# Expert rows of a mixture-of-experts layer: VectorE moves the gathered rows, and the weighted rows get a second buffer

## The chip, the cores and the metric

The kernel runs on one core of a Trainium2 chip. The metric is the device time of one execution in microseconds; the median of three runs is quoted, and beside it one execution that the hardware profiler recorded.

## What is computed

One layer on x, 64 x 64 tokens of 256 numbers (4096 tokens, 32 tiles of 128): cross attention, causal self attention, and a mixture of 8 experts of which each token uses 2, each with its residual. The part that matters here is the last:

```python
logits_BSE = jnp.einsum('BSD,DE->BSE', x, router_kernel_DE)
probs_BSE = jax.nn.softmax(logits_BSE.astype(jnp.float32), axis=-1)
weights_BSK, indices_BSK = jax.lax.top_k(probs_BSE, TOP_K)           # TOP_K = 2 of 8
norm_weights_BSK = jax.nn.softmax(weights_BSK, axis=-1)
...
act_BSEF = jax.nn.silu(jnp.einsum('BSD,EDF->BSEF', x, kernel_gating_EDF))   # D = 256, F = 512
fuse_BSEF = act_BSEF * jnp.einsum('BSD,EDF->BSEF', x, kernel_up_EDF)
down_BSED = jnp.einsum('BSEF,EFD->BSED', fuse_BSEF, kernel_down_EFD)
out_BSD = jnp.einsum('BSED,BSE->BSD', down_BSED, full_weights_BSE)
```

## The kernel before

Both attentions and the router come first and are not touched. After them the tokens are sorted by expert: `token_of` holds, column by column, the token numbers of each tile of 128 rows that one expert handles. There are 67 such tiles, at least 5 for each expert. The expert part then runs over these tiles.

What one tile i needs, in the order of its data:

- a **gather** on GpSimd's queue (`gather(i)`, L1375): an indirect DMA that brings 128 rows of `xn` (256 normalised numbers and the token's 8 expert weights, ROW = 264) from DRAM into one of two buffers `xs_in`. Two small GpSimd instructions stand ahead of it: `token_now` (L1372) copies the tile's token numbers, `dummy` (L1374) waits for that copy.
- a **move** on GpSimd (`move(i)`, L1383 and L1386): the 8 weights go to `slot_weights`, the 256 numbers to the single buffer `e_xs`. The move waits until TensorE has transposed the tile before (`xt_mm`).
- TensorE transposes `e_xs` into `e_xt_ps` (`turn_x(i)`, L1429); ScalarE and VectorE split it into a rounded part and a remainder (`e_xt_hi`, `e_xt_lo`).
- TensorE makes gate and up (`gate_up(i)`, `e_g_ps`, `e_u_ps`, 12 matmuls of 512 columns), ScalarE the silu, VectorE the product `e_h`.
- TensorE transposes `e_h` (`turn_h(i)`, `e_ht_ps`), which is split again (`e_ht_hi`, `e_ht_lo`), and makes the down product `e_y_ps` (`down(i)`, 12 matmuls of 256 columns).
- ScalarE's `y_copy(i)` (L1500) multiplies it by the weights into the single buffer `e_ys`. It waits until the scatter of the tile before has landed (`s_added`), since that scatter reads the buffer.
- a **scatter** on GpSimd's queue (`add_rows(i)`, L1396): an indirect DMA that adds the 128 rows to `acc` in DRAM. `token_out` (L1391) and `out_gate` (L1395) stand ahead of it. Scatters must not overlap, as two experts can add to one row: `token_out` waits for the landing of the scatter before, `out_gate` for `y_copy(i)`.

Each engine works through its own instructions in the order written; semaphores tie them together. TensorE's unit is a step: `step(i)` is turn_x(i+1), turn_h(i-1), gate_up(i), down(i-1). ScalarE's and VectorE's unit is `tile(i)`, with the work that belongs to that step. In the first three steps of each expert but the last, `tile` also splits a third of the next expert's weights (`e_w_hi` on ScalarE, `e_w_lo` on VectorE); when the third is done, the SyncE queue loads the raw weights of the expert after next (three DMAs of 512 KB). GpSimd's loop takes two tiles a turn; for each tile n it does move(n), gather(n+2), add_rows(n-3).

Of the kernel before, what the change touches and what calls it, by code (L numbers as in the profile page):

```python
# [16 lines left out]
ALU = mybir.AluOpType  # L17
# [5 lines left out]
P = 128  # L23
HEAD = 64
MIN_TILES = 5
# [958 lines left out]
def moe(nc, sem, sbuf, psum, xn_sb, xn_dram, s_xn_stored, ident, r_hi, r_lo, w_gate, w_up, w_down, acc,  # L984
# [23 lines left out]
    with ExitStack() as ph:  # L1008
# [288 lines left out]
        with ExitStack() as ex:  # L1297
# [6 lines left out]
            xs_in = [sbuf(ex, f"e_xs_in{i}", [P, ROW]) for i in range(2)]  # L1304
            xs_sb = sbuf(ex, "e_xs", [P, D])
# [6 lines left out]
            ys_sb = sbuf(ex, "e_ys", [P, D])  # L1312
# [54 lines left out]
            def _(pool):  # L1367
                def gather(i, half):


                    wait(pool, s_moved, i - 1 if isinstance(i, int) else i + -1)
                    nc.gpsimd.tensor_tensor(token_now[half][:], token_of[:, bass.ds(i, 1)], none[:], ALU.add).then_inc(s_now, 1)  # L1372
                    pool.wait_ge(s_now, i + 1)
                    nc.gpsimd.tensor_tensor(dummy[half][:], zero[:], zero[:], ALU.add).then_inc(s_dummy, 1)  # L1374
                    pool.indirect_dma_start(  # L1375
                        out=xs_in[half][:], out_offset=None, in_=xn_dram,
                        in_offset=bass.IndirectOffsetOnAxis(ap=token_now[half][:], axis=0)).then_inc(s_xs[half], DMA)

                def move(i, pair, half):

                    pool.wait_ge(s_xs[half], DMA * pair + DMA)
                    wait(pool, s_dummy, i)
                    nc.gpsimd.tensor_tensor(weight[:, bass.ds(i * EXPERTS, EXPERTS)], xs_in[half][:, D:ROW],  # L1383
                                            zero[:].to_broadcast([P, EXPERTS]), ALU.add).then_inc(s_weight, 1)
                    wait(pool, xt_mm, i)
                    nc.gpsimd.tensor_tensor(xs_sb[:], xs_in[half][:, 0:D], zero[:].to_broadcast([P, D]), ALU.add).then_inc(s_moved, 1)  # L1386

                def add_rows(i):
# [8 lines left out]
                        out=acc, out_offset=bass.IndirectOffsetOnAxis(ap=token_out[:], axis=0), in_=ys_sb[:],  # L1397
# [5 lines left out]
                for half in range(2):  # L1403
                    gather(half, half)
                for half in range(2):
                    move(half, 0, half)
                    gather(2 + half, half)
                for half in range(2):
                    move(2 + half, 1, half)
                    gather(4 + half, half)  # L1410
                add_rows(0)
                with pool.Fori(2, more_pairs) as j:
                    for half in range(2):
                        move(2 * j + half, j, half)
                        gather(2 * j + (2 + half), half)
                        add_rows(2 * j + (half - 3))
# [170 lines left out]
```

## Time and profile before

| | us |
|---|---|
| median of 3 runs (lowest, highest) | 2474.48 (2471.78, 2474.54) |
| the profiled execution | 2472.68 |
| its span, first to last instruction | 2470.9 |
| first GpSimd gather, from the span's start | 2060.36 |
| last scatter, from the span's start | 2451.66 |
| last instruction of all, the copy of `acc` to the output | from 2455.55 |

Times in the views below count from the span's start. The expert part, to which the change is confined, is the stretch from 2060 on, some 400 us of the span; all ahead of it is the same in both kernels. "Busy" is the time an engine executed; a duration on GpSimd (POOL) can begin while the instruction before it is still at work, so that its length holds a wait. For a DMA that GpSimd issues, the duration of the instruction is the making of its descriptors, and the rows land later.

### The profile page before, as it was taken

To read this page: it belongs to the slowest core of one execution; us is meant where nothing else is said; L and a number is where in the kernel's file an instruction comes from. 1 tells how busy PE (TensorE), PEld (TensorE's weight loads), DVE (VectorE), ACT (ScalarE), POOL (GpSimd) and SP (SyncE) were. 2 spreads that over 40 slices of the span, in tenths; PEclk is the share of its full clock that TensorE was granted. 3 is DMA by queue.
4 is the path that set the end of the run, shared out by engine and by line. 5 is a ranking of instruction groups with operands and counts; after the bars stand their busy time and mean duration, and the time that the engine had idled before them with its cause. 6 is when DMAs were issued, how large, how long until landed. Compare 5 with 4: busy or idle time off the path is not lost. (4 is left out here: it accounts for less than half of the span.)

```text
span 2470.9 us, 53415 instructions
## 1 busy us (share of the span) xinstructions
PE 2315.3 (94%) x18144; PEld 1993.0 (81%) x18144; DVE 1533.7 (62%) x3324; ACT 1266.8 (51%) x3832; POOL 900.9 (36%) x1141
## 2 busy tenths in 40 slices
PE   6999999999999999999997999999999956998895
PEld 5888888888888888888886889999999844777775
DVE  5656665656565655665555888888888765433332
ACT  4555454545554554555554666666666522433332
POOL 3333333333233323333332222222222224877784
PEclk9999999999999999999998999999999977999998
DMA  5000000000000000000001000000000012334334
GB/s 169 18 10 17 15 10 10 15 17 8 17 8 17 8 17 8 17 8 17 8 1 69 1 18 9 17 17 8 17 8 18 18 37 78 72 74 97 73 48 98
DMA packets 52934, 73.94 MB, mean 30 GB/s; under 512 B 9408, under 2 KB 36800, under 8 KB 52800
## 3 DMA queue, kind: packets, MB, share of 16 engines
q1 hardware_dynamic: 39952, 55.07, 7.0%
q0 software_dynamic: 12912, 17.98, 4.4%
q8 instruction: 38, 0.62, 0.1%
q14 instruction: 32, 0.26, 0.0%
HBM read 55.47 MB, written 21.76 MB: 31 GB/s over the span
## 5 line engine op out<-in xcount | busy, mean ns | idle before, releaser
L356 POOL TENSOR_TENSOR p_sb<-p_sb,rinv 128x512 f32<-128x512 f32 x256 | 283.7, 1108 | 874.0 <-DVE rinv L601 874.0
L523 ACT ACTIVATE p_sb<-s_ps,nmax 128x256 f32<-128x256 f32 x512 | 237.9, 469 | 411.1 <-DVE nmax L582 411.1
L744 POOL TENSOR_TENSOR sp_sb<-sp_sb,srinv 128x512 f32<-128x512 f32 x128 | 133.2, 1041 | 441.7 <-DVE srinv L930 441.7
L57 DVE TENSOR_TENSOR kt_lo<-k_ps,kt_hi 128x512 fp32r<-128x512 f32 x256 | 176.0, 687 | 140.3 <-ACT kt_hi L45 137.6
L58 DVE SCALAR_TENSOR_TENSOR qbd_lo<-m_ps,qbd_hi 64x256 fp32r<-64x256 f32 x256 | 108.0, 422 | 226.9 <-ACT qbd_hi L46 225.2
L45 ACT CAST kt_hi<-k_ps 128x512 fp32r<-128x512 f32 x256 | 150.9, 590 | 169.5 <-PE k_ps L65 169.5
L598 DVE COPY pt_sb<-t_ps 128x512 f32<-128x512 f32 x256 | 176.7, 690 | 43.1 <-PE t_ps L449 39.2
L878 ACT ACTIVATE sp_sb<-sm_sb,snmax 128x128 f32<-128x128 f32 x512 | 199.4, 390 | 6.4 <-DVE snmax L941 3.3
L463 PE MATMUL o_ps<-pt_sb,v_sb 128*64 128x64 f32 x4096 | 175.5, 228 | 0.2 <-DVE pt_sb L598 0.2
L463 PEld LDWEIGHTS o_ps<-pt_sb,v_sb 128*64 128x64 f32 x4096 | 140.1, 137 | 43.5 <-issue 43.2
L582 DVE TENSOR_REDUCE nmax<-s_ps 128x2 f32<-128x512 f32 x256 | 173.9, 679 | 0.0
L57 DVE TENSOR_TENSOR e_ht_lo<-e_ht_ps,e_ht_hi 128x512 fp32r<-128x512 f32 x67 | 46.3, 691 | 187.4 <-ACT e_ht_hi L45 183.3
L449 PEld LDWEIGHTS t_ps<-ident,p_sb 128*128 128x128 f32 x1024 | 127.7, 141 | 34.6 <-issue 0.8
L449 PE MATMUL t_ps<-ident,p_sb 128*128 128x128 f32 x1024 | 153.8, 273 | 0.9 <-DVE pt_sb L598 0.5
L543 ACT COPY v_sb<-v_ps 128x512 f32<-128x512 f32 x256 | 149.7, 585 | 4.8 <-PE v_ps L65 1.7
L65 PE MATMUL s_ps<-kt_hi,qbd_hi 128*128 128x256 f32 x512 | 144.0, 281 | 3.1 <-issue 2.1
L65 PE MATMUL s_ps<-kt_hi,qbd_lo 128*128 128x256 f32 x512 | 144.7, 283 | 0.0
L65 PE MATMUL s_ps<-kt_lo,qbd_hi 128*128 128x256 f32 x512 | 144.6, 282 | 0.0
L65 PE MATMUL k_ps<-cx_hi,wk_hi 128*128 128x512 f32 x256 | 125.9, 492 | 13.1 <-DVE wk_lo L57 8.1
L46 ACT ACTIVATE sqt_hi<-sqk_ps 128x256 fp32r<-128x256 f32 x128 | 49.1, 384 | 155.0 <-PE sqk_ps L65 155.0
L1500 ACT ACTIVATE e_ys<-e_y_ps,slot_weights 128x256 f32<-128x256 f32 x67 | 31.8, 474 | 176.0 <-DMA acc<-e_ys,e_token_out 176.0
L1396 POOL DMA_INDIRECT acc<-e_ys,e_token_out x67 | 107.4, 1603 | 24.2 <-issue 21.4
(278 smaller groups left out, 7607.9 us busy)
## 6 DMA issues: line engine op xcount, KB each, us to landing
ctx_raw<-in_ctx_t SPq DMA_DIRECT2D x32, 256.0 KB, 2.7
ctx_raw<-in_ctx_t SPq DMA_DIRECT2D x64, 128.0 KB, 2.8
xn<-f_xn SPq DMA_DIRECT2D x16, 256.0 KB, 2.2
acc<-x_sb SPq DMA_DIRECT2D x16, 256.0 KB, 2.3
e_raw<-in_gate SPq DMA_DIRECT2D x8, 512.0 KB
e_raw<-in_up SPq DMA_DIRECT2D x8, 512.0 KB
e_raw<-in_down SPq DMA_DIRECT2D x8, 512.0 KB
x_sb<-in_x SPq DMA_DIRECT2D x1, 3584.0 KB, 13.6
```

Source lines behind the costliest of these rows:

```text
L45: return nc.scalar.copy(hi, src)
L57: return nc.vector.tensor_tensor(lo, src, f32(hi), ALU.subtract)
L65: mm = pe.matmul(out, lhs, rhs, start=(i == 0), stop=(i == len(pairs) - 1))
L356: nc.gpsimd.tensor_tensor(prob, prob, inv, ALU.mult).then_inc(norm_done, 1)
L449: mm = pe.transpose(t_ps[:, k * P:(k + 1) * P], p_sb[:, (p - 3) % 4, k * P:(k + 1) * P], ident[:])
L463: mm = pe.matmul(o_ps[h * HEAD:(h + 1) * HEAD, (2 * w + b) * HEAD:(2 * w + b + 1) * HEAD], v_sb[:, k, q * P + h * HEAD:q * P + (h + 1) * H ...
L523: ex = nc.scalar.activation(p_sb[:, k, b * J:(b + 1) * J], s_ps[1 - w][:, b * J:(b + 1) * J], ACT.Exp, bias=nmax[:, k, b:b + 1], scale=1.0 ...
L543: nc.scalar.copy(v_sb[:, p % 4, p // 4 * HALF:(p // 4 + 1) * HALF], v_ps[:]).then_inc(v_done, 1)
L582: nc.vector.tensor_reduce(nmax[:, (p - 1) % 4, :], s_ps[1 - w][:].rearrange("p (b j) -> p b j", b=2), AX_X, ALU.max, negate=True).then_inc ...
L598: nc.vector.tensor_copy(pt_sb[:, 1 - w, :], t_ps[:]).then_inc(t_done, 1)
L744: nc.gpsimd.tensor_tensor(prob, prob, inv, ALU.mult).then_inc(norm_done, 1)
L878: ex = nc.scalar.activation(p_sb[:, s, k * P:(k + 1) * P], sm_sb[:, w, k * P:(k + 1) * P], ACT.Exp, bias=nmax[:, s, k:k + 1], scale=1.0, a ...
```

## The change

- GpSimd's move is gone. VectorE does it (`move(i)`, L1513 to L1521 after): one copy of all 264 columns from `xs_in` to `e_xs`, which now has room for the weights. It waits for the gather's landing, for TensorE's transposes of the tile before, and for ScalarE to have taken the weights of the tile before. It is the last thing VectorE does for a step ahead of any weight split: `tile(i)` ends with move(i+2).
- ScalarE copies the 8 weights from `e_xs` to `slot_weights` behind `e_xt_hi` (L1473).
- `e_ys` is two buffers in turn. `y_copy(i)` no longer waits for the landing of scatter i-1, but for `token_out` of tile i-1, which is behind the landing of scatter i-2.
- GpSimd's loop does, for each tile n, gather(n), add_rows(n-3), where before it was move(n), gather(n+2), add_rows(n-3). Four gathers stand ahead of the loop's first add_rows, where before there were six.

```diff
--- before.py
+++ after.py
@@ -1301,15 +1301,15 @@
             none = sbuf(ex, "e_none", [P, 1], mybir.dt.uint32)
             dummy = [sbuf(ex, f"e_dummy{i}", [P, 1]) for i in range(2)]
             token_out = sbuf(ex, "e_token_out", [P, 1], mybir.dt.uint32)
-            xs_in = [sbuf(ex, f"e_xs_in{i}", [P, ROW]) for i in range(2)]
-            xs_sb = sbuf(ex, "e_xs", [P, D])
+            xs_in = sbuf(ex, "e_xs_in", [P, 2 * ROW])
+            xs_sb = sbuf(ex, "e_xs", [P, ROW])
             xt_hi = sbuf(ex, "e_xt_hi", [P, D], F32R)
             xt_lo = sbuf(ex, "e_xt_lo", [P, D], F32R)
             silu_sb = sbuf(ex, "e_silu", [P, F])
             h_sb = sbuf(ex, "e_h", [P, F])
             ht_hi = sbuf(ex, "e_ht_hi", [P, F], F32R)
             ht_lo = sbuf(ex, "e_ht_lo", [P, F], F32R)
-            ys_sb = sbuf(ex, "e_ys", [P, D])
+            ys = sbuf(ex, "e_ys", [P, 2 * D])
             xt_ps = psum(ex, "e_xt_ps")
             g_ps = psum(ex, "e_g_ps")
             u_ps = psum(ex, "e_u_ps")
@@ -1365,27 +1365,19 @@
             @block.gpsimd
             def _(pool):
-                def gather(i, half):
-
-
-                    wait(pool, s_moved, i - 1 if isinstance(i, int) else i + -1)
+                def gather(i, half, freed):
+
+
+                    wait(pool, s_moved, freed)
                     nc.gpsimd.tensor_tensor(token_now[half][:], token_of[:, bass.ds(i, 1)], none[:], ALU.add).then_inc(s_now, 1)
                     pool.wait_ge(s_now, i + 1)
+                    wait(pool, s_dummy, i)
                     nc.gpsimd.tensor_tensor(dummy[half][:], zero[:], zero[:], ALU.add).then_inc(s_dummy, 1)
                     pool.indirect_dma_start(
-                        out=xs_in[half][:], out_offset=None, in_=xn_dram,
+                        out=xs_in[:, half * ROW:(half + 1) * ROW], out_offset=None, in_=xn_dram,
                         in_offset=bass.IndirectOffsetOnAxis(ap=token_now[half][:], axis=0)).then_inc(s_xs[half], DMA)
-                def move(i, pair, half):
-
-                    pool.wait_ge(s_xs[half], DMA * pair + DMA)
-                    wait(pool, s_dummy, i)
-                    nc.gpsimd.tensor_tensor(weight[:, bass.ds(i * EXPERTS, EXPERTS)], xs_in[half][:, D:ROW],
-                                            zero[:].to_broadcast([P, EXPERTS]), ALU.add).then_inc(s_weight, 1)
-                    wait(pool, xt_mm, i)
-                    nc.gpsimd.tensor_tensor(xs_sb[:], xs_in[half][:, 0:D], zero[:].to_broadcast([P, D]), ALU.add).then_inc(s_moved, 1)
-
-                def add_rows(i):
+                def add_rows(i, half):
                     wait(pool, s_added, DMA * i)
                     nc.gpsimd.tensor_tensor(token_out[:], token_of[:, bass.ds(i, 1)], none[:], ALU.add).then_inc(s_out_now, 1)
@@ -1394,31 +1386,28 @@
                     wait(pool, s_out_gate, i)
                     nc.gpsimd.tensor_tensor(out_gate[:], zero[:], zero[:], ALU.add).then_inc(s_out_gate, 1)
                     pool.indirect_dma_start(
-                        out=acc, out_offset=bass.IndirectOffsetOnAxis(ap=token_out[:], axis=0), in_=ys_sb[:],
+                        out=acc, out_offset=bass.IndirectOffsetOnAxis(ap=token_out[:], axis=0), in_=ys[:, half * D:(half + 1) * D],
                         in_offset=None, compute_op=ALU.add).then_inc(s_added, DMA)
                 more_pairs = pool.value_load(pairs[0:1, 0:1], min_val=MIN_TILES * EXPERTS // 2, max_val=MAX_TILES // 2)
                 nc.gpsimd.memset(none[:], 0).then_inc(s_zero, 1)
                 pool.wait_ge(s_zero, 2)
-                for half in range(2):
-                    gather(half, half)
-                for half in range(2):
-                    move(half, 0, half)
-                    gather(2 + half, half)
-                for half in range(2):
-                    move(2 + half, 1, half)
-                    gather(4 + half, half)
-                add_rows(0)
+                for i in range(4):
+                    gather(i, i % 2, i - 1)
+                add_rows(0, 0)
                 with pool.Fori(2, more_pairs) as j:
                     for half in range(2):
-                        move(2 * j + half, j, half)
-                        gather(2 * j + (2 + half), half)
-                        add_rows(2 * j + (half - 3))
+                        gather(2 * j + half, half, 2 * j + (half - 1))
+                        add_rows(2 * j + (half - 3), 1 - half)
+                left = pool.value_load(first_left[0:1, 0:1], min_val=MIN_TILES * EXPERTS - 4, max_val=MAX_TILES - 4)
                 for half in range(2):
-                    move(2 * more_pairs + half, more_pairs, half)
-                not_added = pool.value_load(first_left[0:1, 0:1], min_val=MIN_TILES * EXPERTS - 4, max_val=MAX_TILES)
-                with pool.Fori(not_added, tile_count(pool)) as i:
-                    add_rows(i)
+                    gather(left + (3 + half), half, left + (2 + half))
+                with pool.Fori(left + 5, tile_count(pool) + 2) as i:
+                    gather(i, 0, left + 4)
+                for k in range(3):
+                    add_rows(left + k, 1 - k % 2)
+                with pool.Fori(left + 3, tile_count(pool)) as i:
+                    add_rows(i, 0)
             @block.tensor
             def _(pe):
@@ -1481,6 +1470,7 @@
                     act.wait_ge(xt_mm, i + 1)
                     wait(act, u_mm, i)
                     split_hi_act(nc, xt_hi[:], xt_ps[:, 0:D]).then_inc(xt_h, 1)
+                    nc.scalar.copy(weight[:, bass.ds(i * EXPERTS, EXPERTS)], xs_sb[:, D:ROW]).then_inc(s_weight, 1)
                 def rest(i):
@@ -1495,9 +1485,8 @@
                 def y_copy(i, e):
                     act.wait_ge(y_mm, i + 1)
-                    act.wait_ge(s_weight, i + 1)
-                    wait(act, s_added, DMA * i)
-                    nc.scalar.activation(ys_sb[:], y_ps[:, 0:D], ACT.Copy,
+                    wait(act, s_out_now, i)
+                    nc.scalar.activation(ys[:, bass.ds((i % 2) * D, D)], y_ps[:, 0:D], ACT.Copy,
                                          scale=weight[:, bass.ds(i * EXPERTS + e, 1)]).then_inc(y_copied, 1)
                 def tile(i, before, e, e_before, piece):
@@ -1522,6 +1511,15 @@
             @block.vector
             def _(dve):
+                def move(i):
+
+                    half = i % 2
+                    dve.wait_ge(s_xs[0], DMA * (i // 2) + DMA)
+                    wait(dve, s_xs[1], DMA * ((i + 1) // 2))
+                    wait(dve, s_weight, i)
+                    wait(dve, xt_mm, i)
+                    nc.vector.tensor_copy(xs_sb[:], xs_in[:, bass.ds(half * ROW, ROW)]).then_inc(s_moved, 1)
+
                 def xt_lo_copy(i):
                     dve.wait_ge(xt_h, i + 1)
                     split_lo_dve(nc, xt_lo[:], xt_ps[:, 0:D], xt_hi[:]).then_inc(xt_l, 1)
@@ -1540,14 +1538,18 @@
                     ht_lo_copy(before)
                     product(i)
                     xt_lo_copy(i + 1)
+                    move(i + 2)
                     if piece is not None:
                         dve.wait_ge(s_whi, PIECES * (e + 1) + piece + 1)
                         cut = slice(piece * CUT, (piece + 1) * CUT)
                         split_lo_dve(nc, w_lo[:, (e + 1) % 2, cut], raw[:, cut], w_hi[:, (e + 1) % 2, cut]).then_inc(s_wlo, 1)
+                move(0)
                 xt_lo_copy(0)
+                move(1)
                 product(0)
                 xt_lo_copy(1)
+                move(2)
                 last = run_tiles(dve, tile)
                 ht_lo_copy(last)
```

The order of GpSimd's instructions in the loop, for the first of a turn's two tiles (n = 2j), before. `e_xs_in` is the landing buffer, `e_xs` the moved rows; a row that only waits or computes an address reads ISA or REGISTER_ALU:

```order
L1383 ISA [waits e_dummy_done]
L1383 TENSOR_TENSOR slot_weights<-e_xs_in,e_zero 128x8
L1386 TENSOR_TENSOR e_xs<-e_xs_in,e_zero 128x256 [waits e_xt_mm]
L35 REGISTER_ALU
L1372 ISA [waits e_xs_moved]
L1372 TENSOR_TENSOR e_token_now<-token_of,e_none 128x1
L1373 REGISTER_ALU
L1374 TENSOR_TENSOR e_dummy<-e_zero 128x1 [waits e_token_now_set]
L1375 DMA e_xs_in<-xn,e_token_now 128x264
L35 ISA
L1391 ISA [waits e_ys_added]
```

And after, from the first row of the loop's body to the wait for the y of tile n-3 and its scatter:

```order
L1372 ISA [waits e_xs_moved]
L1372 TENSOR_TENSOR e_token_now<-token_of,e_none 128x1
L1373 REGISTER_ALU
L1375 TENSOR_TENSOR e_dummy<-e_zero 128x1 [waits e_dummy_done,e_token_now_set]
L1376 DMA e_xs_in<-xn,e_token_now 128x264
L35 ISA
L1383 ISA [waits e_ys_added]
L1383 TENSOR_TENSOR e_token_out<-token_of,e_none 128x1
L1384 REGISTER_ALU
L1387 TENSOR_TENSOR e_out_gate<-e_zero 128x1 [waits e_out_gate_done,e_y_weighted,e_token_out_set]
L1388 DMA acc<-e_ys,e_token_out 4224x256
```

The gather in the loop was that of tile n+2 and stood behind the move of tile n; it is now that of tile n, and stands directly behind the scatter of tile n-4, which is the last row of the turn before.

VectorE's instructions of a step without weight pieces, before:

```order
L57 TENSOR_TENSOR e_ht_lo<-e_ht_ps,e_ht_hi 128x512 [waits e_ht_hi_done]
L1530 REGISTER_ALU
L1533 TENSOR_TENSOR e_h<-e_u_ps,e_silu 128x512 [waits e_ht_mm,e_silu_done,e_u_mm]
L1526 REGISTER_ALU
L57 TENSOR_TENSOR e_xt_lo<-e_xt_ps,e_xt_hi 128x256 [waits e_xt_hi_done]
```

And after:

```order
L1531 TENSOR_TENSOR e_h<-e_u_ps,e_silu 128x512 [waits e_ht_mm,e_silu_done,e_u_mm]
L1524 REGISTER_ALU
L57 TENSOR_TENSOR e_xt_lo<-e_xt_ps,e_xt_hi 128x256 [waits e_xt_hi_done]
L1517 ISA
L35 ISA [waits e_xs_loaded0]
L1521 ISA [waits e_xt_mm,e_weight_kept,e_xs_loaded1]
L1521 COPY e_xs<-e_xs_in 128x264
```

The copy, with two waiting rows of its own, now stands between `e_xt_lo` and the next step's `e_ht_lo`.

## Rows read from the trace of the kernel before

**Rows 1.** GpSimd's timeline (start us, us, what, idle before): scatters of tiles 2, 64.
```profile
2092.38 1.59 POOL L1396 DMA_INDIRECT acc<-e_ys,e_token_out  x1 [0.15 <-issue]
...
2441.22 1.55 POOL L1396 DMA_INDIRECT acc<-e_ys,e_token_out  x1 [0.48 <-issue]
```

**Rows 2.** Windows: us; PE, PEld, DVE, ACT, POOL busy; PEclk, DMA share, GB/s.
```profile
2300.00:2400.00 100.00, 90.72 (x536) 76.13 (x534) 38.24 (x60) 38.92 (x77) 79.76 (x145) 1.00 0.35 64
2430.00:2456.00 26.00, 16.30 (x95) 13.84 (x93) 5.83 (x10) 6.37 (x14) 11.04 (x18) 0.90 0.26 31
```

**Rows 3.** TensorE's timeline, one early step, and the next one's start.
```profile
2079.76 0.38 PE L1429 MATMUL e_xt_ps<-ident,e_xs 128*128 128x128 f32 x2
...
2084.48 0.28 PE L65 MATMUL e_y_ps<-e_w_lo,e_ht_hi 128*128 128x256 f32 x1
2084.59 0.38 PE L1429 MATMUL e_xt_ps<-ident,e_xs 128*128 128x128 f32 x2
```

**Rows 4.** GpSimd's timeline, one tile.
```profile
2206.15 1.61 POOL L1396 DMA_INDIRECT acc<-e_ys,e_token_out  x1 [0.48 <-issue]
2207.22 0.78 POOL L1383 TENSOR_TENSOR slot_weights<-e_xs_in,e_zero 128x8 f32 x1
2207.38 1.19 POOL L1386 TENSOR_TENSOR e_xs<-e_xs_in,e_zero 128x256 f32<-128x256 f32 x1
2208.75 0.19 POOL L1372 TENSOR_TENSOR e_token_now<-token_of,e_none 128x1 uint32<-128x1 uint32 x1 [0.19 <-POOL e_xs L1386]
...
2209.55 1.00 POOL L1375 DMA_INDIRECT e_xs_in<-xn,e_token_now  x1 [0.33 <-issue]
2210.57 0.20 POOL L1391 TENSOR_TENSOR e_token_out<-token_of,e_none 128x1 uint32<-128x1 uint32 x1
2210.84 0.20 POOL L1395 TENSOR_TENSOR e_out_gate<-e_zero 128x1 f32<-128x1 f32 x1
2211.51 1.60 POOL L1396 DMA_INDIRECT acc<-e_ys,e_token_out  x1 [0.48 <-issue]
```

**Rows 5.** The chain that ended last, in order of time: start, us, what.
```profile
2425.26 1.60 POOL acc L1396
2426.86 0.24 POOL slot_weights L1383
...
2428.62 2.76 DMA e_xs_in<-xn,e_token_now
...
2435.99 3.81 DMA acc<-e_ys,e_token_out
```

**Rows 6.** ScalarE's timeline within the stretch of rows 4.
```profile
2210.20 0.47 ACT L1500 ACTIVATE e_ys<-e_y_ps,slot_weights 128x256 f32<-128x256 f32 x1 [2.66 <-DMA acc<-e_ys,e_token_out]
```

**Rows 7.** Waits from 2100 to 2400: us in total, times, longest.
```profile
ACT e_ys L1500 <- DMA acc<-e_ys,e_token_out: 142.5, 53, 5.4
```

**Rows 8.** VectorE's groups by form: busy, mean ns of one.
```profile
L185 DVE TENSOR_SCALAR ln_xn_x<-x_sb,ln_mv_x,ln_rstd_x 128x256 f32 x28 | 20.4, 772 | 0.0
...
L185 DVE TENSOR_SCALAR ln_xn_s<-x_sb,ln_mv_s,ln_rstd_s 128x256 f32 x24 | 8.7, 406 | 0.0
```

**Rows 9.** VectorE's timeline at the step of rows 3.
```profile
2084.02 0.41 DVE L57 TENSOR_TENSOR e_xt_lo<-e_xt_ps,e_xt_hi 128x256 fp32r<-128x256 f32 x1
```

**Rows 10.** GpSimd's timeline: a gather with nothing late ahead of it.
```profile
2076.08 0.19 POOL L1372 TENSOR_TENSOR e_token_now<-token_of,e_none 128x1 uint32<-128x1 uint32 x1
...
2076.68 0.97 POOL L1375 DMA_INDIRECT e_xs_in<-xn,e_token_now  x1
```

**Rows 11.** The chain that ended last, at two of the expert weight loads.
```profile
2060.36 5.55 DMA e_xs_in<-xn,e_token_now
...
2228.40 6.38 DMA acc<-e_ys,e_token_out
```

**Rows 12.** VectorE's and GpSimd's timelines at a weight piece.
```profile
2224.87 1.45 DVE L57 TENSOR_TENSOR e_w_lo<-e_raw,e_w_hi 128x1024 fp32r<-128x1024 f32 x1 [0.38 <-ACT e_w_hi L45]
...
2225.39 0.97 POOL L1372 TENSOR_TENSOR e_token_now<-token_of,e_none 128x1 uint32<-128x1 uint32 x1 [0.17 <-POOL e_xs L1386]
```

## The prediction

> **What bounds the kernel now.** The times by step come first. The expert part is one pipeline over 67 tiles, so I read it at its pace. Between the starts of the scatters of tiles 2 and 64 lie 2441.22 - 2092.38 = 348.84 us for 62 tiles, 5.63 us each [rows 1]. The windows say how hard each engine works in there: in 100 us TensorE is busy 90.7 and GpSimd 79.8, VectorE 38 and ScalarE 39, at a granted clock of 1.00, which is TensorE's upper level, 2.4 GHz [rows 2]. TensorE looks like the bound, but its own work is shorter than the pace: in an early step, when the first gathers had run ahead, it goes from one `turn_x` to the next in 2084.59 - 2079.76 = 4.83 us [rows 3]. So some 0.8 us a tile is waiting, about 50 us over the part, and that is the most that any relief could give.
>
> GpSimd's timeline says what sets the pace. From one scatter to the next, 2206.15 to 2211.51, it runs one instruction behind the other: scatter, the two moves, `token_now`, `dummy`, gather, `token_out`, `out_gate`, scatter, in 5.36 us [rows 4]. The "busy" 80% is an undercount, since the rest is hand-over between its own instructions, 0.2 to 0.5 us at a time. Beside it stands a ring through the single `e_ys`: the scatter lands 3.81 us after its start [rows 5], and only then may ScalarE write the next `e_ys`, from which the next scatter starts 2211.51 - 2210.20 = 1.31 us later [rows 4, 6]. That makes 5.1 to 5.3 us, nearly the same pace; it is what the 142.5 us of waiting ahead of `e_ys` are [rows 7]. Both must be relieved for a gain, and the change relieves both.
>
> **What is removed.** The moves leave GpSimd. Their real end is 2208.57 (2207.38 + 1.19), and the scatter ahead of them is done at 2207.76 [rows 4], so they occupy about 0.8 us, and with the wait on them ahead of `token_now` about 1 us. GpSimd's round would be 5.36 - 1.0 = 4.4 us. The ring no longer holds `e_ys`: landing, `token_out`, `out_gate`, scatter, which is 3.81 + about 0.1 + (2211.51 - 2210.57 = 0.94) = 4.85 us at most. Both lie at TensorE's 4.83.
>
> **What is added on VectorE and ScalarE.** VectorE gets one copy of 128x264 a tile, from SBUF to SBUF. The trace has no such copy. The nearest row is a VectorE operation of 128x256 f32 with an SBUF source and no second tensor, 406 ns; the same operation takes 772 ns in the stage where something holds it up [rows 8]. Below, a copy at twice the element rate would be some 0.2 us. I take 0.35 and keep 0.2 and 0.77 for the range. The Trainium skill ("VectorE: DVE Perf Modes", section "Mode 2×_2P") says that an fp32 copy between SBUF tensors handles two elements per cycle; by its clock and its overheads that is an estimate of 0.2 to 0.3 us, and the sum would be some 3 us lower by it. No row here shows such a copy.
>
> The copy stands behind `e_xt_lo`, which ends at 2084.02 + 0.41 = 2084.43, 0.16 before TensorE starts the next `turn_x` at 2084.59 [rows 3, 9]. With the copy and a hand-over of 0.15 TensorE could start at 2084.93: 0.33 us late. So even with every gather early the pace would be 4.83 + 0.33 = 5.16, not 4.83. ScalarE's copy of 8 weights (about 0.2 us) lies between `e_xt_hi` and `y_copy` while TensorE is still at the down product, 1.4 us; I cost it at nothing. With the weight pieces, 21 of 67 steps, that cover is used up and it would cost its 0.2 us each, 4 us at most.
>
> **What is moved: the gather.** This decides, in my reading. Before, GpSimd did gather(n+2) in the round of tile n, so a gather stood behind the scatter of a tile six before its own, and its landing was never late. After, gather(n) is in the round of tile n, directly behind scatter n-4. That scatter waits in `out_gate` for y_copy(n-4), and y_copy(n-4) for the down product of tile n-4, which is the last work of TensorE's step n-3. The gathered rows are wanted by turn_x(n) at the start of step n-1. So only step n-2 lies between the event that frees the gather and the moment its rows are needed, and the way from one to the other is long. Link by link, from the end of the down product:
>
> - hand-over to ScalarE 0.15 (as from ScalarE to GpSimd: 2210.84 less 2210.67 = 0.17 [rows 4, 6]);
> - start of y_copy to start of the scatter 1.31 [rows 4, 6];
> - the scatter's descriptors 1.60, and the first small instruction behind it 0.24 [rows 5]; here that is `token_now`;
> - end of `token_now` to the start of the gather, 2076.68 - 2076.27 = 0.41, as nothing late stands ahead [rows 10];
> - start of the gather to its landing 2.76 [rows 5];
> - hand-over to VectorE 0.15, the copy 0.35, hand-over to TensorE 0.15.
>
> The sum is L = 7.12 us. TensorE then needs, from the start of that step to the end of its down product, 2084.48 + 0.28 - 2079.76 = 5.00 us [rows 3]. The loop closes over two steps: end of step n-3, L, start of step n-1, 5.00, end of step n-1. So two steps take 7.12 + 5.00 = 12.12 us, and the pace is 6.06, if nothing else is slower. TensorE will wait for the moved rows 1.2 us a step on the mean, likely short and long by turns, since a step that follows a long wait finds its own gather nearly there.
>
> Against 5.63 now that is 0.43 us a tile more, over 62 tiles 27 us. Three smaller terms. The loads of expert weights, one for each of 7 experts, stretch what is under way beside them: a gather from 2.76 to 5.55 us and a scatter from 3.81 to 6.38 [rows 5, 11]. The pace of before holds such delays already; the 6.06 does not. As the two interleaved chains can absorb part of a delay, I add 1 us for each, under half of the 2.6 to 2.8: 6 us. The weight pieces: while VectorE makes `e_w_lo`, a GpSimd instruction of 0.19 us takes 0.97 [rows 10, 12]. Before, that was in the 5.63 as well; afterwards it falls on the chain above in part of the 21 cases, 0.8 us at every fourth or fifth: 3 us. At the ends something is saved: the first move is 0.35 instead of about 0.8, and for the last tiles no gather is left, so the ring of 4.85 instead of 5.2 holds for three scatters, and the start is a little quicker: -5 us. The sum is 27 + 6 + 3 - 5 = 31 us. The profiled execution took 2472.68 us, 1.8 below the median of the runs; 2472.7 + 31 = 2503.7, and I say 2503.
>
> **The rivals.** A measurement of this kernel can tell about 0.2%, 5 us, from no change.
>
> *The gather is in time* (faster; 0.10). What speaks for it is what the diff removes, since both limits of before go. Then VectorE's late copy sets 5.16: 62 x 0.47 = 29 us less, 2444. It needs a way from down product to rows of at most 5.3 us, where I count 7.12; the descriptors of scatter and gather and the landing alone are 1.60 + 2.76 = 4.36. The point from which it turns: at L = 6.26 the pace equals today's, at about 5.8 the other terms are paid too and the kernel is faster by more than 5 us.
>
> *Late, but for no more than was lost before* (no change; 0.07). L near 6.1 to 6.2 gives a pace of 5.55 to 5.6, and 2470 to 2479 with the smaller terms. It would take hand-overs of 0.05 us, a copy of 0.2 and a gather that lands 2.3 us after its start.
>
> *VectorE's copy holds GpSimd off* (slower still; 0.15). When TensorE has waited, the copy falls 1.4 to 1.8 us after the end of the down product, which is when GpSimd starts the scatter's descriptors. VectorE and GpSimd do get in each other's way at `e_w_lo`, 0.19 against 0.97 us [rows 10, 12]. If each copy adds its 0.35 to L, the pace rises by 0.17, 11 us in all: 2514. The Trainium skill speaks against this change here: "SBUF — State Buffer", section "SBUF: two separate sides", has it that an fp32 copy from SBUF to SBUF on VectorE keeps GpSimd from writing descriptors while it runs. The row agrees for an operation with two SBUF inputs, and shows nothing for a copy.
>
> *TensorE's clock* (0.08). With a wait of 1.2 us a step TensorE is busy 4.83 of 6.06, 80%. At 63% busy (16.3 of 26 us, in the last tiles) the clock granted was 0.90; at 91% it was 1.00 [rows 2]. If it were 0.95 throughout, the 5.00 in the loop would be 5.26: 62 x 0.13 = 8 us more, 2511.
>
> **The numbers.** The late gather as summed has 0.60; with the two rivals that lie above it, 0.83 are slower. Its ends: a gather landing after 2.4, a copy of 0.2 and hand-overs of 0.1 make L = 6.46, a pace of 5.73, +6 us, and with half of the small terms 2480. A copy of 0.77, a landing of 3.1 and 0.35 for the hold-off make L = 8.23, 6.6 and +61, which all at once is unlikely; two of the three give about 2528. The forecast's own range is 2486 to 2522. For 8 in 10 I give 2476 to 2530, which leaves out the faster rival and the far upper end.
>
> **What would show it.** In the changed profile: the pace of scatters about 6.06 us; TensorE's largest wait in the part that for `e_xs` by VectorE (1 to 1.3 us a step), and behind it VectorE's copy waiting for the gather's DMA, about as long; GpSimd waiting in `out_gate` for ScalarE's `e_ys`; hardly any wait of `e_ys` for a landing. If instead VectorE's copy waits for `e_xt_lo` alone and the pace is 5.2, the gather was in time and I am wrong. Wrong too would be a pace of 6 with the chain leading through landings of scatters.

## The result, and the profile after

The changed kernel takes 2564.96 us (2561.35 to 2570.36) against 2474.16 (2471.78 to 2474.54) for the kernel before on the same chip. The ratio is 1.0371, with an interval of 1.0349 to 1.0393: slower by about 91 us. The forecast was 2503 us, so the direction was right and the size a third of what came.

GpSimd's timeline after (columns as in [rows 1]), the scatters of tiles 2 and 64:

```profile
2091.87 1.59 POOL L1388 DMA_INDIRECT acc<-e_ys,e_token_out  x1 [0.15 <-issue]
...
2539.54 1.59 POOL L1388 DMA_INDIRECT acc<-e_ys,e_token_out  x1 [0.50 <-issue]
```

447.67 us for 62 tiles is 7.22 us a tile, where [rows 1] gave 5.63. That is 98.8 us more, so the whole loss lies in the pace of the expert part: the two profiled executions, 2472.68 and 2570.36, are 97.7 apart.

The two rows of the waits from 2100 to 2500 that matter (engine, what it waited for: us in total, times, longest):

```profile
PE e_xt_ps L1418 <- DVE e_xs L1521: 78.2, 29, 5.0
DVE e_xs L1521 <- DMA e_xs_in<-xn,e_token_now: 70.3, 28, 5.0
```

TensorE waits for VectorE's copy of the gathered rows, and VectorE for the gather to land. The number of times is what to read: 29 and 28 in some 56 steps. Every second step waits, for 78.2 / 29 = 2.7 us, and the others hardly at all. The 142.5 us of `e_ys` for a landing [rows 7] have no row any more.

The same on TensorE's timeline, where each row is a `turn_x`, the start of a step:

```profile
2306.14 0.68 PE L1418 MATMUL e_xt_ps<-ident,e_xs 128*128 128x128 f32 x2 [2.29 <-DVE e_xs L1521]
...
2312.73 0.43 PE L1418 MATMUL e_xt_ps<-ident,e_xs 128*128 128x128 f32 x2
...
2320.18 0.43 PE L1418 MATMUL e_xt_ps<-ident,e_xs 128*128 128x128 f32 x2 [2.35 <-DVE e_xs L1521]
...
2325.40 0.43 PE L1418 MATMUL e_xt_ps<-ident,e_xs 128*128 128x128 f32 x2
```

Two steps do the same work, and both follow a wait of 2.3 us. The one from 2320.18 takes 5.22, the one from 2306.14 takes 6.59. The windows say why (us; PE, PEld, DVE, ACT, POOL busy; granted clock, DMA share, GB/s): first four of 100 us each, then the stretch of those steps, with what lies between left out:

```profile
2100.00:2200.00 100.00, 80.74 (x399) 68.60 (x400) 33.44 (x58) 33.62 (x72) 46.96 (x80) 0.84 0.30 66
2200.00:2300.00 100.00, 83.54 (x422) 70.20 (x421) 31.80 (x59) 32.29 (x73) 46.31 (x83) 0.86 0.28 53
2300.00:2400.00 100.00, 80.59 (x425) 68.56 (x424) 35.94 (x63) 36.10 (x77) 49.43 (x85) 0.90 0.27 53
2400.00:2500.00 100.00, 79.54 (x425) 67.79 (x424) 32.08 (x60) 33.20 (x74) 48.71 (x86) 0.90 0.28 53
...
2306.00:2309.00 3.00, 2.86 (x10) 2.57 (x11) 0.68 (x2) 0.59 (x1) 2.46 (x4) 0.50 0.41 49
2310.00:2313.00 3.00, 2.96 (x20) 2.53 (x19) 1.45 (x4) 1.98 (x5) 0.00 (x0) 1.00 0.00 0
...
2320.00:2324.00 4.00, 3.83 (x21) 3.29 (x22) 1.97 (x4) 1.24 (x3) 2.92 (x5) 1.00 0.39 51
```

TensorE has stood still for 2.3 us; then the granted clock is 0.50, which is its lower level of 1.2 GHz, for the next 3 us. It is back at 1.00 by 2310. Behind the wait that ends at 2320 it does not fall. The kernel before had 1.00 throughout this part and 0.90 only at its end [rows 2]. Of the 400 us here, (0.16 + 0.14 + 0.10 + 0.10) / 0.5 x 100 = 100 us were at the lower level. In windows of 2 us over 2090 to 2550 it is 109 us, with TensorE busy for 97 of them. Half of that work time, 48 us, is a first estimate of what the clock cost. Counted on TensorE's timeline it is a little less: from the step at 2099.99 on, 32 steps follow a wait of 1.9 us or more, and 27 of them take 6.4 to 7.8 us from their start to the end of their down product, where all other steps take 5.1. The excess of the 27 adds up to 45 us.

The chain of waits over one long wait of TensorE (start, us, what). It follows the end of the down product, 2312.69, and ScalarE's `e_ys`, which starts at 2312.96:

```profile
2313.57 0.52 POOL e_out_gate L1387
...
2314.28 0.06 POOL acc L1388
...
2315.36 0.74 POOL e_token_now L1372
...
2316.51 2.74 DMA e_xs_in<-xn,e_token_now
...
2319.28 0.11 DVEq L35
...
2319.44 0.05 DVEq L35
...
2319.54 0.11 DVEq L1521
...
2319.70 0.35 DVE e_xs L1521
...
2320.18 0.43 PE e_xt_ps L1418 x2
```

This is the way that the prediction counted out, link for link: gate, scatter, `token_now`, gather, landing, copy, `turn_x`.

### The profile page after: what moved, and what is told of

Its sections match the earlier page's. It is cut to its first block and busy times, and to the rows that moved or that the text cites. A ratio compares the mean times of both kernels' runs of the same rounds, so it can differ in the third digit from the quotient of the medians.

```text
span 2568.6 us, 53602 instructions
## 1 busy us (share of the span) xinstructions
PE 2359.1 (92%) x18144; PEld 2031.0 (79%) x18144; DVE 1551.7 (60%) x3393; ACT 1285.3 (50%) x3900; POOL 838.6 (33%) x1008
## 5 line engine op out<-in xcount | busy, mean ns | idle before, releaser
L1418 PE MATMUL e_xt_ps<-ident,e_xs 128*128 128x128 f32 x136 | 33.9, 336 | 101.4 <-DVE e_xs L1521 99.2
L1531 DVE TENSOR_TENSOR e_h<-e_u_ps,e_silu 128x512 f32<-128x512 f32 x67 | 46.3, 691 | 130.9 <-PE e_u_ps L65 130.9
L1388 POOL DMA_INDIRECT acc<-e_ys,e_token_out x67 | 106.7, 1593 | 30.0 <-issue 29.4
```

## The experiments

All times are medians, each with the kernel before timed beside it; "ratio" is the time over that of the kernel before, with its 95% interval. The diffs are cut to the lines that matter, and "..." marks where lines were left out.

### The gather one tile earlier

Everything of the change is kept; only the gather is brought forward in GpSimd's order.

```
-                for i in range(4):
+                for i in range(5):
                     gather(i, i % 2, i - 1)
...
-                        gather(2 * j + half, half, 2 * j + (half - 1))
+                        gather(2 * j + (half + 1), 1 - half, 2 * j + half)
                         add_rows(2 * j + (half - 3), 1 - half)
```

> The kernel after, with one thing moved: in GpSimd's loop the gather of tile n+1 stands where that of tile n stood, ahead of the scatter of tile n-3, so five gathers instead of four run ahead of the first scatter. Theory (the late gather): the moved rows are there when TensorE wants them; the waits for e_xs of 2.3 us in every other step go, the granted clock stays at 1.00, and the pace falls from 7.22 us a tile to what VectorE's copy behind e_xt_lo allows, 5.2 to 5.3, which gives 2445 to 2458 us. Rival (the copy on VectorE itself, its place on the path or its hold on GpSimd, is what costs): the order of the gathers changes little, pace above 6.5, 2520 us or more.

Measured: 2445.99 us (2443.32 to 2449.87) against 2473.04, ratio 0.9896 (0.988 to 0.9913). One place in the queue turns 91 us of loss into 27 of gain. Its window, its waits for the copy from 2100 to 2400, and two starts of steps:

```profile
2200.00:2300.00 100.00, 97.45 (x575) 83.10 (x575) 47.12 (x83) 47.28 (x103) 67.41 (x115) 1.00 0.40 82
```
```profile
PE e_xt_ps L1417 <- DVE e_xs L1520: 4.0, 12, 0.6
```
```profile
2181.87 0.43 PE L1417 MATMUL e_xt_ps<-ident,e_xs 128*128 128x128 f32 x2
...
2187.06 0.43 PE L1417 MATMUL e_xt_ps<-ident,e_xs 128*128 128x128 f32 x2
```

TensorE is busy 97.5%, the clock is 1.00, and a step takes 5.19 us. That the late gather is the cause of all of the loss, the clock's part too, is shown by this: nothing else was changed.

### Matmuls that nobody reads ahead of each step

To learn what the clock is worth in the changed kernel, TensorE gets work to do while it would wait. The kernel computes the same; 5 or, in a second kernel, 8 extra matmuls go to a PSUM bank that nothing reads.

```
                 def step(i, before, w, w_before):
+                    for _ in range(5):
+                        pe.matmul(fill_ps[:], w_hi[:, w, 0:P], w_hi[:, w, 0:F], start=True, stop=True)
                     turn_x(i + 1)
```

> The kernel after, with five matmuls of 512 columns into an unused PSUM bank at the start of each TensorE step, some 1.17 us of work that nothing reads. Theory (two costs in one: the late gather, and behind each long wait about 3.5 us at the clock's lower level): the filler takes the place of half of each long wait, so TensorE is never idle for 2.3 us, the granted clock stays near 1.00, and the loop over two steps falls from 14.4 us to 7.4 + 5.0 = 12.4 us, a pace of 6.2: 2565 - 62 x 1.02 = 2502 us, faster by more work. Rival (the clock is not a cost of its own, the 14.4 us are waits on the chain): the filler is hidden at best, 2560 to 2570 us, or comes on top, up to 2565 + 36 = 2600 us.

> The kernel after with eight filler matmuls a step in place of five, 1.87 us of work that nothing reads, so that TensorE's step has 6.70 us of work. Theory (the lower clock behind a wait of 2.3 us and more is what costs, and with it some 1.7 us of every second step): plain steps never wait, also the waits beside the weight loads stay under 2.5 us and the clock stays up, pace 6.75: 2565 - 62 x 0.47 = 2536 us, less than with five fillers, by more work. Rival (five fillers took away all that the clock costs, and more filler is only more work): 2546 + 62 x 0.4 = 2570 us.

Measured: with 5, 2546.15 us (2545.6 to 2548.45), ratio 1.03 (1.0282 to 1.0317); with 8, 2560.44 us (2559.96 to 2563.08), ratio 1.0353 (1.0337 to 1.0369). Some starts of steps with 5:

```profile
2108.11 0.38 PE L1419 MATMUL e_xt_ps<-ident,e_xs 128*128 128x128 f32 x2
...
2120.91 0.38 PE L1419 MATMUL e_xt_ps<-ident,e_xs 128*128 128x128 f32 x2
...
2134.21 0.43 PE L1419 MATMUL e_xt_ps<-ident,e_xs 128*128 128x128 f32 x2 [0.27 <-DVE e_xs L1523]
...
2143.57 0.43 PE L1419 MATMUL e_xt_ps<-ident,e_xs 128*128 128x128 f32 x2 [3.11 <-DVE e_xs L1523]
...
2151.22 0.38 PE L1419 MATMUL e_xt_ps<-ident,e_xs 128*128 128x128 f32 x2
```

and the windows of its plain stretch and of the one beside a weight load:

```profile
2107.00:2139.00 32.00, 30.64 (x175) 25.70 (x175) 13.24 (x23) 13.47 (x28) 18.66 (x29) 1.00 0.29 57
2139.00:2150.00 11.00, 7.89 (x38) 6.37 (x37) 2.15 (x5) 2.13 (x5) 3.57 (x7) 0.84 0.48 124
```

In the plain stretch two steps take 12.8 us here (2108.11 to 2120.91) and 12.5 on most others, though each carries 1.2 us more work; without the extra matmuls the usual pair took 14.1. So there the clock made the last 1.5 us of the 14.1: more work took less time. The other 12.6 are the way through the gather, as a pair without the fall of the clock shows below. Beside a load the gather is later still: the step from 2134.21 takes 9.4 us, 3.1 of them the wait at its end, the clock falls behind it, and the next step takes 7.6. The result, 2546, is neither the 2502 of the theory nor the 2560 and more of the rival. Six steps beside the loads still run in part at the lower clock (7.4 to 7.7 us), which costs some 9 us, so about 36 of the 45 us of the clock were removed, and yet only 19 came back in the median, and 25 between the two profiled executions. Where the rest went was not traced. So no run takes the clock's part away alone, and the 45 us stay a count from the trace.

With 8 the plain steps take 6.72 us by their own work, at 1.00, and around the loads waits of 1.9 to 2.3 us stay, four of the five with a lower clock behind them. One of them (two windows, and the starts of two steps):

```profile
2100.00:2200.00 100.00, 94.71 (x524) 80.49 (x523) 34.39 (x61) 35.10 (x76) 51.96 (x85) 0.98 0.33 72
2145.00:2150.00 5.00, 5.00 (x18) 4.06 (x19) 0.69 (x1) 1.18 (x2) 2.43 (x5) 0.66 0.33 53
```
```profile
2144.95 0.43 PE L1419 MATMUL e_xt_ps<-ident,e_xs 128*128 128x128 f32 x2 [2.03 <-DVE e_xs L1523]
...
2153.29 0.38 PE L1419 MATMUL e_xt_ps<-ident,e_xs 128*128 128x128 f32 x2
```

Over these 100 us TensorE is busier than in the kernel before, 94.7% against 90.7% [rows 2], and behind one wait of 2.03 us the clock falls all the same: the step takes 8.34 us in place of 6.72. The mean share of busy time does not tell the two apart. The 8 matmuls gained less than the 5 because they make the plain steps longer than the gather needs, and still do not reach the waits beside the loads. Neither of the two times I had named for this kernel came out.

### The loads of expert weights made small

From the third expert on only 3 x 64 KB are loaded in place of 3 x 512 KB, so later experts work with weights that are mostly those of others: a part of the loading is left out.

```
         def load_expert(sp, e):
+            if e > 1:
+                for k, w in ((0, w_gate), (1, w_up), (2, w_down)):
+                    sp.dma_start(raw[:, k * GU:k * GU + 128], w[e, 0:P, 0:128]).then_inc(s_raw, DMA)
+                return
```

> The kernel after, with the loads of the expert weights from expert 2 on cut to three DMAs of 64 KB in place of three of 512 KB; the later experts then work on weights that are partly left over, so this leaves out a part of the computation. Theory (a load beside the gathers delays a landing on the chain that TensorE waits for): the steps of 9.6 to 10.2 us that come once per expert in the kernel after fall to the usual 7.4, six times 2.3 us and for the first load nothing, 2565 - 14 = 2551 us, with the pairs of 14.1 us unchanged. Rival (the loads were hidden, or cost only the 1 us each that the prediction had): 2558 to 2565 us.

Measured: 2547.12 us (2546.34 to 2550.63) against 2471.79, ratio 1.0299 (1.0282 to 1.0316), 18 us less than the changed kernel. The steps of 9.6 to 10.2 us beside the loads are gone; the rest is as it was. Every second start of a step:

```profile
2142.21 0.62 PE L1422 MATMUL e_xt_ps<-ident,e_xs 128*128 128x128 f32 x2 [2.42 <-DVE e_xs L1525]
...
2156.37 0.68 PE L1422 MATMUL e_xt_ps<-ident,e_xs 128*128 128x128 f32 x2 [2.31 <-DVE e_xs L1525]
...
2170.30 0.43 PE L1422 MATMUL e_xt_ps<-ident,e_xs 128*128 128x128 f32 x2 [2.26 <-DVE e_xs L1525]
...
2182.95 0.43 PE L1422 MATMUL e_xt_ps<-ident,e_xs 128*128 128x128 f32 x2 [2.43 <-DVE e_xs L1525]
```

and two of its windows:

```profile
2156.00:2159.00 3.00, 2.63 (x10) 2.35 (x11) 0.68 (x2) 0.59 (x1) 2.65 (x4) 0.50 0.38 44
2170.00:2175.00 5.00, 4.70 (x29) 4.16 (x30) 2.98 (x6) 2.12 (x5) 2.84 (x5) 1.00 0.34 53
```

This trace shows the two kinds of pairs cleanly: 2142.21 to 2156.37 is 14.16 us, with the clock down behind the wait, and 2170.30 to 2182.95 is 12.65, without. Mostly two pairs of the first kind follow each other, and then one of the second. Of the 31 steps behind a long wait 21 are slow, and their excess over 5.1 us adds up to 31 us, where the changed kernel had 45. The two profiled executions, 2570.36 and 2550.63, are 19.7 us apart: 14 of them are clock, and the other 6 can be put to the longer landings themselves.

### The kernel before with two buffers for the weighted rows

The one part of the change that touches neither the moves nor the gathers, done alone.

```
-            ys_sb = sbuf(ex, "e_ys", [P, D])
+            ys = sbuf(ex, "e_ys", [P, 2 * D])
...
-                    wait(act, s_added, DMA * i)
-                    nc.scalar.activation(ys_sb[:], y_ps[:, 0:D], ACT.Copy,
+                    wait(act, s_out_now, i)
+                    nc.scalar.activation(ys[:, bass.ds((i % 2) * D, D)], y_ps[:, 0:D], ACT.Copy,
```

> The kernel before, with the second e_ys buffer alone; GpSimd still moves. Theory (both limits must be relieved: GpSimd's own round of 5.36 us stays): same as before within 5 us, 2466 to 2475 us, while ScalarE's wait for the landing is gone. Rival (the ring through the single e_ys was the limit): pace near 5.0, 2440 us or less.

Measured: 2459.34 us (2458.76 to 2463.44), ratio 0.9951 (0.9934 to 0.9968), 14 us faster. I had expected no change, as GpSimd's round of 5.36 us would stay. It did not stay; its timeline:

```profile
2202.99 1.61 POOL L1396 DMA_INDIRECT acc<-e_ys,e_token_out  x1
...
2207.68 0.20 POOL L1395 TENSOR_TENSOR e_out_gate<-e_zero 128x1 f32<-128x1 f32 x1
2208.02 1.60 POOL L1396 DMA_INDIRECT acc<-e_ys,e_token_out  x1
```

From gate to scatter it is 0.34 us, where [rows 4] show 2211.51 - 2210.84 = 0.67, and the round is 5.03. The two limits were not independent: with `e_ys` ready in time, 0.33 us of the round that I had read as GpSimd's own are gone. They lie between the gate and the scatter. Why a gate that came late is followed by a longer gap was not tested.

### The early gather with one buffer's waits

```
-                    wait(act, s_out_now, i)
+                    wait(act, s_added, DMA * i)
```

> As the kernel with the gather one place earlier, but y_copy waits again for the landing of the scatter of the tile before, as if e_ys were one buffer; GpSimd's round is short, the ring through e_ys is as before. Theory: the ring of 3.81 + 1.31 + about 0.15 = 5.27 us sets the pace, and the late landings beside the weight loads cost as before, some 2 us each: 2455 to 2470 us, so 5 to 15 us behind the kernel with both. Rival (the second buffer earns nothing once GpSimd is free, as VectorE's late copy sets 5.2 anyway): within 4 us of the kernel with the earlier gather.

Measured: 2474.22 us (2471.19 to 2475.2), ratio 1.0002 (0.9992 to 1.0011). Its row of waits, to be laid beside [rows 7]:

```profile
ACT e_ys L1488 <- DMA acc<-e_ys,e_token_out: 142.4, 51, 5.2
```

With the moves gone from GpSimd and the gathers early, but the ring through `e_ys` back, nothing is gained at all: I had expected 3 to 18 us. The second buffer alone is worth 14 us, the freed GpSimd (with the copy on VectorE in its place) 0, both 27.

### Shortening TensorE's way to the next step

Three kernels build on the one with the early gather. The first lets VectorE copy ahead of `e_xt_lo`. The second also makes `token_out` double, so that only the gate waits for a landing, and lets `y_copy` wait for the gate of the tile before in place of its `token_out`. The third also takes ScalarE's weight copy ahead of `e_xt_hi`, and VectorE's copy ahead of the product `e_h`.

```
-                    xt_lo_copy(i + 1)
                     move(i + 2)
+                    xt_lo_copy(i + 1)
```
```
-                    wait(pool, s_added, DMA * i)
-                    nc.gpsimd.tensor_tensor(token_out[:], ...
+                    nc.gpsimd.tensor_tensor(token_out[half][:], ...
                     pool.wait_ge(s_out_now, i + 1)
                     pool.wait_ge(y_copied, i + 1)
+                    wait(pool, s_added, DMA * i)
...
-                    wait(act, s_out_now, i)
+                    wait(act, s_out_gate, i)
```
```
                     act.wait_ge(xt_mm, i + 1)
+                    nc.scalar.copy(weight[:, bass.ds(i * EXPERTS, EXPERTS)], xs_sb[:, D:ROW]).then_inc(s_weight, 1)
                     wait(act, u_mm, i)
                     split_hi_act(nc, xt_hi[:], xt_ps[:, 0:D]).then_inc(xt_h, 1)
...
                     ht_lo_copy(before)
-                    product(i)
                     move(i + 2)
+                    product(i)
```

> The kernel with the gather one place earlier, and VectorE's copy ahead of e_xt_lo instead of behind it. Theory (with early gathers the copy behind e_xt_lo is what TensorE waits for, 0.3 us in each step): TensorE's step falls from 5.18 to about 4.85 us in plain steps, and then the scatters' ring of 4.8 to 4.9 us with its late landings beside the weight loads, 7.1 to 7.7, sets a mean of about 5.1: 2436 to 2442 us, 5 to 10 us less than with the earlier gather alone. Rival (the second e_ys absorbs the late landings, so TensorE's own 4.83 shows): 2425 us.

> The one before, with two token_out buffers, so that token_out is made ahead of the landing of the scatter before, and only out_gate waits for it. Theory (the ring landing, token_out, out_gate, scatter is then the limit): the ring loses the 0.27 us of token_out, 4.85 to 4.6, and makes up for late landings sooner: 2428 to 2434 us. Rival (TensorE's own 4.83 us a step and not the ring): the same as the one before within 3 us.

> The kernel with early gathers, the copy first and two token_out buffers, with VectorE's copy now ahead of the product of the same step, and ScalarE's copy of the weights ahead of e_xt_hi so that this is possible. Theory (transposes wait for e_xt_lo as well as for e_xs, so with the copy on either side of e_xt_lo the work between the up product and the next step, product, copy and e_xt_lo, is 0.3 us too long; only taking the copy out of that stretch helps): plain steps fall from 5.18 to 4.85 us, 62 x 0.3 = 18 us less, 2428 to 2434 us, if the gather has landed when the copy is due, some 3 us into the step. Rival (it has not in most steps, and now the product waits behind the copy): 2450 us or more.

Measured, in this order: 2448.58 us (2447.43 to 2451.45), ratio 0.9904 (0.9888 to 0.9921); 2447.63 us (2446.18 to 2449.3), ratio 0.99 (0.9883 to 0.9916); 2432.93 us (2430.39 to 2433.45), ratio 0.9836 (0.9823 to 0.985). The first two are where the early gather alone was. Why, shows VectorE's timeline of the first:

```profile
2189.03 0.30 DVE L1520 COPY e_xs<-e_xs_in 128x264 f32 x1
2189.24 0.42 DVE L57 TENSOR_TENSOR e_xt_lo<-e_xt_ps,e_xt_hi 128x256 fp32r<-128x256 f32 x1
```

The next `turn_x` starts at 2189.71, behind `e_xt_lo` as it was behind the copy: it writes the one `e_xt_ps`, so it waits for whichever of the two is last. Changing their order changes nothing; my theory had left that wait out. In the second kernel TensorE still took 5.17 us a step, while scatters that had fallen behind a weight load caught up at 4.37 us each, so the scatters were no longer the limit. The third moves the copy away from `e_xt_lo`, into time in which VectorE was idle; its rows on VectorE and TensorE:

```profile
2183.89 0.39 DVE L1520 COPY e_xs<-e_xs_in 128x264 f32 x1 [0.94 <-ACT slot_weights L1470]
2184.36 0.69 DVE L1530 TENSOR_TENSOR e_h<-e_u_ps,e_silu 128x512 f32<-128x512 f32 x1
2184.96 0.41 DVE L57 TENSOR_TENSOR e_xt_lo<-e_xt_ps,e_xt_hi 128x256 fp32r<-128x256 f32 x1
```
```profile
2180.71 0.38 PE L1417 MATMUL e_xt_ps<-ident,e_xs 128*128 128x128 f32 x2
...
2185.58 0.38 PE L1417 MATMUL e_xt_ps<-ident,e_xs 128*128 128x128 f32 x2
```

GpSimd's timeline in the third, where it catches up:

```profile
2218.39 0.19 POOL L1387 TENSOR_TENSOR e_out_gate<-e_zero 128x1 f32<-128x1 f32 x1 [2.73 <-DMA acc<-e_ys,e_token_out]
2218.73 1.59 POOL L1388 DMA_INDIRECT acc<-e_ys,e_token_out  x1
...
2222.63 0.19 POOL L1387 TENSOR_TENSOR e_out_gate<-e_zero 128x1 f32<-128x1 f32 x1 [0.45 <-DMA acc<-e_ys,e_token_out]
2223.11 1.59 POOL L1388 DMA_INDIRECT acc<-e_ys,e_token_out  x1 [0.28 <-issue]
```

A step is 4.87, TensorE's own 4.83 of [rows 3] at last. From scatter to scatter it is 2223.11 - 2218.73 = 4.38 us, and the second gate has waited 0.45 for the landing of the scatter before: what paces the scatters here is that landing, not GpSimd's own work. The kernel is 40 us faster than before and 132 faster than the change.

## Why the prediction was wrong, and what of it was right

The step that failed is the clock: a lower clock behind the waits stood in the prediction as a rival at 8 us, and not in the sum; the runs show it as some 45 us. A second term, the length L of the way through the gather with the step behind it, was too small by 0.45 us a pair of steps, 14 us in all. The mechanism itself, the late gather, was right.

**Two limits before, both relieved.** Right in the main: neither part alone reached what both did (14, 0 and 27 us). But "both must be relieved for a gain" was too strong, since the second buffer alone gave 14; 0.33 us of GpSimd's 5.36 belonged to the ring. GpSimd's own round after was put at 4.4. The 4.38 of the last kernel looks like it, but that is luck, as it holds a wait of 0.45 for a landing; GpSimd's own part is shorter, by an estimate from those rows about 3.9. The ring of landings, put at 4.85 at most, is what shows as 4.38 there, with `token_out` taken out of it.

**VectorE's copy.** Taken as 0.35 us; it took 0.32 on the mean (63 of the copies, 20.0 us), nearer to the estimate of 0.2 to 0.3 from the Trainium skill ("VectorE: DVE Perf Modes", "Mode 2×_2P") than to the 0.77 of [rows 8]. The pace with early gathers, 4.83 + 0.33 = 5.16, was right: 5.19 in the first experiment, and the faster rival's 2444 is that experiment's 2446. What the rival missed is only that the change does not issue the gathers early enough.

**The late gather.** The step that decides was right in kind and nearly in size. From the trace after, from the end of the down product at 2312.69 to `turn_x` at 2320.18: 0.27 to ScalarE's `e_ys`, 1.32 to the scatter, 1.82 to the end of `token_now`, 0.41 to the gather, 2.74 to the landing, 0.45 to the copy, 0.35 for it and 0.13 to TensorE. That is L = 7.49 where I summed 7.12. The step behind it, up to the end of its down product, took 5.08, not 5.00. The two together are 12.57 where I had 12.12: 31 pairs at 0.45 are 14 us. Most of it is the link from landing to copy, 0.45 in place of 0.15. The queue's rows in the chain (DVEq) show three small instructions there, 0.27 us with 0.10 between them. They stand at the lines where VectorE's waits compare with a value in a register; that this is what makes them necessary was not tested. Long and short steps by turns were as foretold.

**The clock.** This is the term that failed. The prediction had: "If it were 0.95 throughout, the 5.00 in the loop would be 5.26: 62 x 0.13 = 8 us more", as a rival with 0.08. It took the 80% busy as one number and the 0.90 at 63% as its neighbour. The trace has idle stretches of 2.3 us by turns, and behind 27 of the 32 long ones some 3 us at the lower level, on the very path that the loop closes over: a step of 6.7 in place of 5.1. The price was about 45 us, not 8, and it adds to the late gather rather than standing beside it. I had treated it as a rival to the sum when it was a consequence of it.

**VectorE holds GpSimd off.** Not for this copy. The scatter's descriptors take 1593 ns on the mean of 67, as in [rows 5], and 1591 to 1594 in the kernels with early gathers. They do overlap: in the last kernel 64 of 67 scatters overlap a copy. The gathers are not longer either: in the first experiment 20 of them overlap a copy and take 0.99 us, as do those that overlap nothing. The rule of the Trainium skill that I had weighed ("SBUF — State Buffer", "SBUF: two separate sides") does not show as longer descriptors here. Beside `e_w_lo` it is otherwise: in the first experiment 15 gathers overlap one, and take 1.3 us on the mean and up to 1.89.

**Loads, weight pieces, ends.** The loads' own part was about 6 us by the small-load experiment, as foretold, and their clock part 14, which no term held. The weight pieces' 3 us were not tested; in the changed kernel no gather is issued beside an `e_w_lo`. The ends gave 97.7 - 98.8 = -1 us, not -5.

Together, against the profiled execution: 31 summed, 14 for the longer L, 45 for the clock and 4 for the ends are 94 us, measured 97.7. As the 45 are counted from the trace and the 14 from one pair, the sum is good to some 5 us, no better. The forecast's own 31 us fit in it, though its 3 us for the weight pieces were not tested; what it lacked is the clock, half of the loss.

What stays open: what lets the clock fall behind one wait of 2.3 us and not behind the next of 2.35. The neighbouring rows are alike in both cases, and no run here separates them.

## What to carry to other kernels

An operation moved to a free engine leaves its place in the old queue; look at what else stands in that queue and moves with it. Here one place of the gather decided between 27 us gained and 91 lost. If the sum says that TensorE will wait, cost the clock behind the wait too, as a part of the sum: look at the single wait's length, and not only at the mean share of busy time (with TensorE 94.7% busy the clock fell behind a wait of 2.03 us, and at 90.7% with waits of at most 1.5 us it stayed). And a gain ends at the next wait of the same instruction: `turn_x` waits for the copy and for `e_xt_lo`, both on VectorE, and to change their order paid nothing; only taking the copy out of that stretch did.

## What the runs showed of the hardware

- TensorE's granted clock was 0.50 for some 3 us behind 27 of 32 waits of 1.9 to 5.0 us that came every 13 to 17 us (behind 21 of 31 with the small loads), while [rows 2] show 1.00 at 90.7% busy with waits of at most 1.5 us. At about 2 us both are seen: with 8 unread matmuls the clock fell behind a wait of 2.03 us, and in the kernel before it stayed at 1.00 behind one of the same length, which ended at 2236.66. Filling the wait with unread matmuls kept it at 1.00 away from the weight loads, and two steps with 2.4 us more work went from 14.1 to 12.5 us.
- A VectorE copy of 128x264 f32 between SBUF buffers, 0.3 us, did not lengthen the descriptors of a scatter (1.59 us) or of a gather (0.99) that it overlapped; `e_w_lo`, with two SBUF inputs and 1.2 us, went with gathers of up to 1.89 us.
- A scatter starts 0.34 us after its gate in the kernel where `e_ys` was ready in time, and 0.67 to 0.71 where the gate had waited for ScalarE's `e_ys`. A wait alone does not make the difference: after a gate that had waited 2.73 us for a landing (2218.39 in the last kernel) it was 0.34 too. What does is not shown.
- In the chain above, VectorE's copy started 0.45 us after the landing of the gather that it waited for.
